# Delta stage of a small Perceiver block: triangular solve by doublings, filters as matrix products

## The reference, cut to what matters

```
q, k, v = silu(conv4(hs @ Wq)), silu(conv4(hs @ Wk)), silu(conv4(hs @ Wv))   # causal, per channel
beta = sigmoid(hs @ Wb);  q, k = l2norm(q), l2norm(k)                     # per head
A = tril_strict((k * beta) @ k.T);  u = inv(I + A) @ (v * beta) ...       # chunks of 32, state S
delta = tril(q @ k.T) @ u                                                 # the same, unchunked
local_short, local_long = fir5(v), fir64(v)                               # causal, per channel
stats = [mean, var, mean|.|, l2] of local_short, local_long, delta, v     # 16 per token and head
logits = gelu([hs, stats] @ mlp_w1 + b1) @ mlp_w2 + b2;  p = softmax(logits / temp) * 0.84 + floor
o = p0 * local_short + p1 * local_long + p2 * delta + p3 * v + sigmoid(res) * local_short
out = (o * rsqrt(mean(o * o) + 1e-5) * rms_w) @ Wo
```

## Time and profile before

| | us |
|---|---|
| three runs | 453.78, 455.37, 457.92 (median 455.37) |
| the profiled execution | 456.18 |
| its span | 454.1 |
| start of the delta stage (xn turned, L696) | 393.42 |
| x after it (L1648) | 439.13 |

### The profile page before, as it was taken

The page is one execution under the profiler, slowest core; times in us unless marked ns, Lnnn a source line. Parts: engine busy times, 40 slices in busy tenths (PEclk is TensorE's granted clock), DMA queues, the critical chain, the costliest instruction groups (busy, mean ns, idle before and its releaser), DMA issues.

```text
span 454.1 us, 11496 instructions
## 1 busy us (share of the span) xinstructions
PE 406.9 (90%) x4493; PEld 321.3 (71%) x4493; DVE 341.5 (75%) x927; ACT 286.5 (63%) x558; POOL 220.4 (49%) x141
## 2 busy tenths in 40 slices
PE   6988999999989999989888999999999999874776
PEld 3956777777767788889656776777776889753575
DVE  2688888888877886447599989888888764488653
ACT  3366888888878876334187897988898651260220
POOL 1177879878845620010014698874665100169110
PEclk9799999999999999999999999999999999995989
DMA  8689897989999889600049999999999900000000
GB/s 321 254 230 177 146 168 134 178 155 219 167 227 238 178 149 398 243 0 5 1 89 192 168 191 191 188 174 193 197 188 194 157 4 1 1 0 0 2 0 3
DMA packets 185781, 64.95 MB, mean 143 GB/s; under 512 B 181168, under 2 KB 181376, under 8 KB 184960
## 3 DMA queue, kind: packets, MB, share of 16 engines
q1 hardware_dynamic: 185440, 63.18, 70.2%
q10 hardware_dynamic: 288, 1.05, 0.7%
HBM read 18.76 MB, written 0.03 MB: 41 GB/s over the span
## 4 chain that ended last, share of the span: by engine, by line
PE 32%; DVE 31%; POOL 10%; ACT 8%; issue 8%; DMA 8%; SPq 2%; DVEq 0%; POOLq 0%; ACTq 0%
DVE probs L563 13%; PE ps L475 9%; DMA probsT<-halves 7%; PE ps L443 7%; PE ps L690 4%; ACT probs L507 4%; POOL halves L539 3%; DVE probsT L592 3%; ACT halves L514 2%; DVE U L581 2%; POOL moe L1244 2%; PE ps L455 2%; PE ps L976 2%; SPq L395 2%; DVE den L576 1%
## 5 line engine op out<-in xcount | busy, mean ns | idle before, releaser
L539 POOL TENSOR_TENSOR halves<-probs,halves 128x896 f16<-128x896 f32 x67 | 126.5, 1891 | 83.4 <-ACT halves L514 82.6
L443 PE MATMUL ps<-ctxT_parts,GT_parts 128*128 128x512 f16 (+1 forms) x672 | 145.4, 353 | 11.5 <-DVE negmax L563 9.5
L475 PE MATMUL ps<-ctxN,probsT 128*128 128x128 f16 x2352 | 149.3, 219 | 6.5 <-DMA probsT<-halves 4.0
L475 PEld LDWEIGHTS ps<-ctxN,probsT 128*128 128x128 f16 x2352 | 139.2, 98 | 21.0 <-issue 6.1
L507 ACT ACTIVATE probs<-probs,shifted 128x896 f32<-128x896 f32 x112 | 115.5, 1032 | 12.3 <-DVE shifted L568 12.3
L443 PEld LDWEIGHTS ps<-ctxT_parts,GT_parts 128*128 128x128 f16 x672 | 60.2, 98 | 63.8 <-DVE negmax L563 14.3
L514 ACT CAST halves<-probs 128x896 f16<-128x896 f32 x92 | 84.9, 923 | 0.1
L563 DVE CUSTOM_DVE_ANT_0 probs<-ps,zero,negmax 128x896 f32<-128x896 f32 x56 | 67.5, 1205 | 1.5 <-PE ps L443 1.3
L563 DVE CUSTOM_DVE_ANT_0 probs<-ps,maskb,negmax 128x896 f32<-128x896 f32 x56 | 67.5, 1205 | 1.2 <-POOL halves L539 0.7
L581 DVE SCALAR_TENSOR_TENSOR U<-U,alpha,ps 128x128 f32<-128x128 f32 x112 | 38.4, 343 | 32.8 <-PE ps L475 32.6
L690 PE MATMUL ps<-cst 128*128 128x128 f32 x454 | 61.5, 286 | 0.0
(11 more groups left out here) (347 smaller groups left out, 388.8 us busy)
## 6 DMA issues: line engine op xcount, KB each, us to landing
moe<-in_ctxT SPq DMA_DIRECT2D x7, 448.0 KB, 8.1
moe<-in_mask SPq DMA_DIRECT2D x6, 448.0 KB, 10.8
moe<-in_gateT SPq DMA_DIRECT2D x2, 1024.0 KB, 9.3
moe<-in_upT SPq DMA_DIRECT2D x2, 1024.0 KB, 10.8
moe<-in_downT SPq DMA_DIRECT2D x2, 1024.0 KB, 12.7
probsT<-halves SPq DMA_TRANSPOSE x92, 4.7
wv<-in_wv SPq DMA_DIRECT2D x2, 512.0 KB, 4.9
wo<-in_wo SPq DMA_DIRECT2D x2, 512.0 KB, 5.7
```

The source lines that it names most:

```text
L443: ins = pe.matmul(ps[:, 2 * b + h, 0:width], GT_parts[:, g_part, r * P:(r + 1) * P], ctxT_parts[:, keys:keys + width], start=(g_part == 0 ...
L475: ins = pe.matmul(ps[:, bank, 0:D], probsT_parts[:, b, p_part, k * P:(k + 1) * P], ctxN_parts[:, at:at + D], start=(p_part == 0 and c_part ...
L539: eng.tensor_tensor(halves_of(L, n)[:, 1, :], probs[:, n % BUFS, :], halves_of(L, n)[:, 0, :], ALU.subtract).then_inc(lower_of(L, n)[0], 1)
```

## The change

The convolution's taps are multiplied into Wq, Wk and Wv by one GpSimd product, so that q, k and v come out of 12 products over shifted columns of xn (`conv`). The solve uses two partition halves of 64 tokens, two heads each: six levels, in each of which TensorE multiplies the right-hand side and the key matrix by one factor (`hop_x`) and the next factor out of the key matrix (`hop_y`); ScalarE copies the one, VectorE the other under a mask. The filters are products with diagonal matrices that are loaded after the second attention pass (`fir`), the long one spread between the levels by `FIR_AT`. Branches lie on 128 partitions (64 tokens, two sides of two heads), 64 columns each, and the statistics of v and the short filter are taken between the levels, those of the delta and the long filter after them. Tanh takes the place of Exp for beta, and Silu's table is asked for ahead. On GpSimd the identity copy for the factors is at step 30 of the second pass, the weights' product after it. Cut to its core:

```
 
 GATE_BANKS, DOWN_BANKS = (2, 3, 4, 5), (6, 7, 0, 1)
 WARM = [0, 2, 6, 6, 6, 6]
...
 for _name, _width in [("ident", P), ("ones", P), ("block32", P), ("later", S), ("upto", S), ("head8", AH),
...
+            pe.wait_ge(sem("d_convw"), 1)
+
+            def conv(i, bank, col):
+                for k in range(TAPS):
+                    for side in range(2):
+                        rows = slice(side * S, (side + 1) * S)
+                        ins = pe.matmul(ps[rows, bank, col:col + S], conv_w[:, i, k, rows], xpad[:, k:k + S],
+                                        start=(k == 0), stop=(k == TAPS - 1))
+                return ins
+
+            def fir(first, last):
+                for k in range(first, last):
+                    for side in range(2):
+                        rows = slice(side * S, (side + 1) * S)
+                        ins = pe.matmul(ps[rows, 7, 0:S], vpad[rows, k:k + S], fir_long[rows, k, :], start=(k == 0),
+                                        stop=(k == FIR_L - 1))
+                return ins
...
+            def by_head(bank, left, right):
+                for h in range(DH):
+                    dims, side = slice(h * DD, (h + 1) * DD), h // 2
+                    ins = pe.matmul(ps[side * S:(side + 1) * S, bank + h % 2, 0:S], left[dims, :], right[dims, :],
+                                    start=True, stop=True)
+                return ins
+
+            def hop_y(level):
+                for a in range(2):
+                    for side in range(2):
+                        rows = slice(side * S, (side + 1) * S)
+                        ins = pe.matmul(ps[rows, 1, a * S:(a + 1) * S], X[rows, a, DD:], LT[rows, level, a, :],
+                                        start=True, stop=True)
+                ins.then_inc(sem("d_hop"), 1)
...
+            def hop_x(level, right, width):
+                for a in range(2):
+                    for side in range(2):
+                        rows = slice(side * S, (side + 1) * S)
+                        ins = pe.matmul(ps[rows, 0, a * width:(a + 1) * width], LT[rows, level, a, :],
+                                        right[rows, a, 0:width], start=True, stop=True)
+                return ins
...
+            conv(0, 0, 0)
+            conv(1, 0, S).then_inc(sem("d_given"), 1)
+            for side in range(2):
+                rows = slice(side * S, (side + 1) * S)
+                pe.matmul(ps[rows, 1, S:2 * S], W("wb")[:, rows], xpad[:, TAPS - 1:], start=True, stop=True)
+            conv(2, 1, 0).then_inc(sem("d_given"), 1)
+            stay_warm(pe, 6, 2)
+            pe.wait_ge(sem("d_dve"), D_DVE["sq"])
+            pe.matmul(ps[:, 2, 0:2 * S], C("block32"), sq, start=True, stop=True).then_inc(sem("d_given"), 1)
...
+            pe.wait_ge(sem("d_act"), D_ACT["v"])
...
+            for side in range(2):
+                rows = slice(side * S, (side + 1) * S)
+                pe.matmul(ps[rows, 6, 0:S], vpad[rows, FIR_L - 1:], ident[rows, rows], start=True, stop=True)
...
+                    rows = slice(side * S, (side + 1) * S)
+                    at = FIR_L - FIR_S + k
+                    ins = pe.matmul(ps[rows, 6, S:2 * S], vpad[rows, at:at + S], fir_short[rows, k, :], start=(k == 0),
+                                    stop=(k == FIR_S - 1))
+            ins.then_inc(sem("d_given"), 1)
...
+            for side in range(2):
+                rows = slice(side * S, (side + 1) * S)
+                ins = pe.matmul(ps[rows, 5, 0:S], R[rows, :], ident[rows, rows], start=True, stop=True)
+            ins.then_inc(sem("d_given"), 1)
+            fir(0, FIR_AT[0])
+            pe.wait_ge(sem("d_dve"), D_DVE["kbeta"])
+            by_head(3, qkh[:, 1, :], kbneg).then_inc(sem("d_given"), 1)
+            by_head(0, kbneg, qkh[:, 1, :]).then_inc(sem("d_given"), 1)
+            fir(FIR_AT[0], FIR_AT[1])
+            for level in range(LEVELS - 1):
+                pe.wait_ge(sem("d_lt"), level + 1)
...
+                hop_y(level)
+                hop_x(level, X, DD + S if level < LEVELS - 2 else DD).then_inc(sem("d_hop"), 1)
+                if level == 0:
+                    pe.wait_ge(sem("d_dve"), D_DVE["qhat"])
+                    by_head(3, qkh[:, 1, :], qkh[:, 0, :]).then_inc(sem("d_given"), 1)
+                fir(FIR_AT[level + 1], FIR_AT[level + 2])
+            pe.wait_ge(sem("d_lt"), LEVELS)
+            pe.wait_ge(sem("d_x"), LEVELS)
+            hop_x(LEVELS - 1, w, DD).then_inc(sem("d_given"), 1)
+            fir(FIR_AT[LEVELS], FIR_AT[LEVELS + 1])
+            pe.wait_ge(sem("d_dve"), D_DVE["bm"])
+            pe.wait_ge(sem("d_x"), LEVELS + 1)
...
+                    ins = pe.matmul(ps[rows, 2, a * DD:(a + 1) * DD], Bm[rows, a, :], u_s[rows, a, :], start=True,
+                                    stop=True)
+            ins.then_inc(sem("d_given"), 1)
+            fir(FIR_AT[LEVELS + 1], FIR_L).then_inc(sem("d_given"), 1)
+            stay_warm(pe, 0, 8)
...
+            pe.matmul(ps[:, 4, 0:DH * S], d_w[:, 4 * D:5 * D], xpad[:, TAPS - 1:].unsqueeze(1).broadcast_to([P, DH, S]),
+                      start=True, stop=False)
+            pe.wait_ge(sem("d_stats"), 2)
...
-            pe.matmul(ps[:, 1, 0:S], W("wb"), xnT[:, 0:S], start=True, stop=True).then_inc(sem("d_given"), 1)
...
-            for g in range(8):
...
-                pe.matmul(ps[:, g, 0:8 * w], C("block32"), Z[:, g, 0:8 * w], start=True,
...
-                pe.matmul(ps[0:S, 2, D:2 * D], firp[:, :, k], ident, start=(k == 0), stop=(k == 3))
...
-
...
-            for g in range(1, 8):
-                key_products(pool, g).then_inc(sem("d_z"), 1)
...
-            pseq(pool.tensor_tensor(firp[:, :, 0:rest], windows(vpad, rest),
-                                    W("fir_l")[:, 0:rest].unsqueeze(1).broadcast_to([P, S, rest]), ALU.mult))
...
-            while width > 4:
-                pseq(pool.tensor_tensor(firp[:, :, 0:width], firp[:, :, 0:width], firp[:, :, width:2 * width], ALU.add))
...
+                        if n == 30:
+                            pool.tensor_copy(LT.rearrange("p l a t -> p (l a) t"),
+                                             C("pairs")[:, 0:S].unsqueeze(1).broadcast_to([P, 2 * LEVELS, S])).then_inc(
+                                sem("d_lt_ident"), 1)
+                    loaded(pool, "delta", "conv")
+                    pool.wait_ge(sem("o1T_ready"), 1)
+                    pool.tensor_tensor(conv_w, conv_w, d_w[:, 0:3 * D].rearrange("p (i d) -> p i d", i=3).unsqueeze(
+                        2).broadcast_to([P, 3, TAPS, D]), ALU.mult).then_inc(sem("d_convw"), 1)
...
+            act.activation(sres[:, 1, :], W("res"), ACT.Exp, scale=-1.0).then_inc(sem("d_early"), 1)
+            loaded(act, "delta")
+            act.activation(w1s[:], w1s[:], ACT.Copy, scale=C("w1scale", slice(0, 16))).then_inc(sem("d_early"), 1)
...
-            act.activation(vpad[:, FIR_L - 1:], cv[:, 2, :], ACT.Silu).then_inc(sem("d_v"), 1)
-            act.wait_ge(sem("d_nrm"), 1)
-            act.activation(rn.rearrange("p a t -> p (a t)"), nrm, ACT.Sqrt).then_inc(sem("d_sqrt"), 1)
...
-            for k in range(FIR_L - ACT_TAPS, FIR_L):
-                a = PARAM["fir_l"][0] + k
-                act.activation(firp[:, :, k], vpad[:, k:k + S], ACT.Copy,
-                               scale=par[:, a:a + 1]).then_inc(sem("d_taps"), 1)
...
+            act.activation(spare[:], C("power"), ACT.Silu)
...
+            act.activation(qkc.rearrange("p a t -> p (a t)"), ps[:, 0, 0:2 * S], ACT.Silu).then_inc(sem("d_act"), 1)
...
+            act.activation(vpad[:, FIR_L - 1:], ps[:, 1, 0:S], ACT.Silu).then_inc(sem("d_act"), 1)
+            act.activation(tb, ps[:, 1, S:2 * S], ACT.Tanh, scale=0.5).then_inc(sem("d_act"), 1)
+            act.wait_ge(sem("d_given"), D_GIVEN["norm"])
+            act.activation(rn.rearrange("p a t -> p (a t)"), ps[:, 2, 0:2 * S], ACT.Sqrt,
...
+            act.wait_ge(sem("d_given"), D_GIVEN["vb"])
+            act.copy(X[:, :, 0:DD], ps[:, 5, 0:S].rearrange("p (a d) -> p a d", a=2))
+            act.wait_ge(sem("d_given"), D_GIVEN["gram"])
+            act.copy(X[:, :, DD:], ps[:, 0:2, 0:S]).then_inc(sem("d_x"), 1)
+            for level in range(LEVELS - 2):
+                act.wait_ge(sem("d_hop"), 2 * level + 2)
+                act.copy(X.rearrange("p a c -> p (a c)"), ps[:, 0, 0:2 * (DD + S)]).then_inc(sem("d_x"), 1)
+            act.wait_ge(sem("d_hop"), 2 * LEVELS - 2)
+            act.copy(w.rearrange("p a c -> p (a c)"), ps[:, 0, 0:2 * DD]).then_inc(sem("d_x"), 1)
             act.wait_ge(sem("d_brcopied"), 1)
...
-            act.activation(st[:, :, :, 3].rearrange("p h b -> p b h"),
-                           mom[:, 2, :].rearrange("p (b h) -> p b h", b=4), ACT.Sqrt).then_inc(sem("d_stats"), 1)
+            act.activation(sqs[:, 0:2, :], br[:, 0:2, :], ACT.Square).then_inc(sem("d_squares"), 1)
+            act.wait_ge(sem("d_given"), D_GIVEN["u"])
```

(91 more changed lines are left out.)

297 lines of the change are left out of this document (105 added, 192 removed).

## The result

| | before | after |
|---|---|---|
| median of four runs, us | 456.41 | 437.97 |
| lowest and highest | 453.78, 457.92 | 437.51, 438.64 |
| the profiled execution, and its span | 456.18, 454.1 | 437.51, 435.4 |
| xn turned (start) | 393.42 | 392.66 |
| transposes of the statistics (start) | 429.50 | 411.52 |

The ratio of after to before is 0.9603 [0.9552, 0.9654]. Between the profiled executions 18.7 us are gone: 17.9 in the stage (46.00 us from xn turned to the addition's end, now 28.07), and 0.76 ahead of it.

The account below looks back on a forecast made before the run. Two chains ending together, GpSimd's long filter and VectorE's substitution, were taken as the bound. 18.8 us gained, less 0.3 for the identity copy and 0.5 for tile switches, gave 18.0: 456.18 to 438.2, range 434.5 to 445.5.

Parts of the forecast that it names:

- kbneg ready: End of the convolution and norm part: kbneg at 399.0 where the old kernel has 401.25, 2.2 us gained.
- Diagonal tiles: Filter products on TensorE: two 64x64 tiles laid diagonally overlap, 0.117 us a pair, with 0.23 kept for the range.
- rival of 448.8: Filter pairs on TensorE: diagonal tiles go one after the other at 0.23 a pair, 10.6 us together; chance 0.08.
- that of 470: Filter pairs between levels: tiles in series at the low clock, 0.46 a pair, slower than before; chance 0.03.
- Tile shapes: TensorE's switches of tile shape, five on the path: 0 to 0.5 us, 0.5 taken.
- Tanh and Silu's table: ScalarE in the convolution: tanh needs no table load (0, else 1.28); loading Silu's table ahead covers 1.28 us.
- Shortening one alone would give nothing: Old delta stage: GpSimd's filter chain and VectorE's substitution end together, so cutting only one gains nothing.
- The change removes both: Old delta stage: the change takes away both GpSimd's filter chain and VectorE's 63 substitution steps.
- rival of 446: TensorE from level 0 on: the clock falls, doubling the same terms, some 8 us; chance 0.05.
- Moved work: Identity copy in the second pass 0 to 1.6 us, 0.3 taken; weights' product 3.1, hidden; added loads nothing.
- Levels: Solve's levels: 1.2 us each from products, latency, ScalarE's copy and hand-overs, with five filter pairs free.
- rival of 442: Levels and statistics: slower hand-overs, 0.5 us more a level and 1 in the statistics; chance 0.14.

Follow-up runs that it names:

- a_byside: Changed kernel with the long filter's products issued all of side 0, then all of side 1, per group: 0.976 of the kernel before, 445.25 us, stage 4.48 longer.
- a_tail: Changed kernel with 46 of the long filter's 64 pairs behind the last level: 0.9726 of the kernel before, stage 34.76 us, 4.87 longer.
- a_nosilu: Changed kernel without the early request for Silu's table: 0.9613 of the kernel before, stage 29.88 us, no change.
- b_nofilter: Kernel before without GpSimd's multiply for 48 long-filter taps and its additions by halves: ratio 0.9999, stage 47.23 us, 0.59 shorter.
- b_half: Kernel before with 31 of the 63 substitution steps: ratio 1.0077, stage 50.38 us, 2.56 longer.
- b_both: Kernel before with 31 of 63 substitution steps and without GpSimd's 48 long-filter taps: ratio 0.9972, stage 45.74 us, 2.08 shorter.
- b_order: b_both with TensorE's branch products ahead of its last substitution wait, 18 idle products between, four later ones removed: 0.9837 of the kernel before, 447.44 us, stage 38.60.
- a_onetap: Changed kernel with one tap of the long filter instead of 64: 0.9617 of the kernel before, stage 30.29 us, 0.40 longer.
- b_half_warm: Kernel before with 31 substitution steps, full filter, b_order's TensorE order and 48 idle products: ratio 1.0063, stage 47.52 us, 0.30 shorter.
- a_onetap_warm: Changed kernel with one long-filter tap and idle products (five before the products by head, two per level): 0.9609 of the kernel before, stage 28.93 us, 0.96 shorter.

## Why the prediction was right

The forecast was 438.2, measured 437.97. By its own steps, with its clock (xn turned and ready at 393.75) moved back by 0.72, to 393.03, where the copy of xn starts in the changed kernel:

| step | predicted | measured |
|---|---|---|
| kbneg ready | 398.28 | 398.28 |
| products by head start | 398.63 | 398.96 |
| first level starts | 399.88 | 399.89 |
| period of a level | 1.20 | 1.28 |
| u copied | 406.7 | 407.03 |
| statistics ready | 410.43 | 410.93 |
| transposes, with the 0.5 for tile shapes | 411.28 | 411.52 |
| transposes to the addition's end, less than before | 0.8 | 0.71 |

The mechanism is right, but the last few tenths are luck. The stage was forecast to lose 18.3 us (18.8 less 0.5) and lost 17.93; ahead of it 0.3 more was forecast, and 0.76 less came, which scatter explains as well (last section). Inside the stage, the products by head start 0.33 late, and the first level starts 0.93 behind them, not 1.25: their records are shorter than the 0.06 us allowed (16 in 0.46 us). The two errors cancel in the third row.

- **Diagonal tiles.** Right, and the step that decides. 72 filter records, all of them into bank 7, both halves of the partitions, take (2.27 - 0.22) / 71 = 0.029 each, 0.115 a pair, where 0.117 was taken. a_byside shows the other end of the range, 0.056 for neighbours on one tile, and what it costs: 4.48 us of the stage. The Trainium skill's rule (TensorEngine Tiling (Array Packing), Gotcha 1) that different row tiles cannot access one PSUM bank at the same time does not hold for tiles that differ in rows and columns: the measurement decides. The rival of 448.8 fell with it, and that of 470.
- **Tile shapes.** The last of 72 filter records began at 396.76 + 2.27 - 0.22 = 398.81 and the products by head 0.15 later, where neighbours of one shape follow at 0.03: 0.12 for a change between tiles of 64 and of 32 rows. Three such changes lie on the path: one ahead of the products by head, two in the first level, where TensorE's queue has no gap. That is 0.36, inside the range of 0 to 0.5, of which the upper end was taken. The one behind the products by head is off the path: the first level waits for VectorE's masked copy and starts 0.94 behind the products by head in a_tail too, which has no filter there.
- **Tanh and Silu's table.** Tanh needed no load: right. That the early request covers 1.28 us: **wrong**, as a_nosilu shows; nothing is lost without it.
- **The bound of the old kernel.** "Shortening one alone would give nothing": right, by b_nofilter and by b_half, which even lost. "The change removes both", as the full reason: **incomplete**. b_both removes both and gains 2 us. The change gains 18 because it also takes away TensorE's own chain of branch products behind its wait for the substitution, and the low clock in which they ran; b_order, with half the substitution and all of that out of the way, gets 9.2, 7.1 of them by the third chain. Of the other 8.7, 8.0 lie ahead of the transposes (27.85 us after the power that begins the stage in b_order, 19.86 in the changed kernel), 2.2 of them in the convolution: kbneg is ready 6.62 after that power, 8.84 in the kernel before, the 2.2 of the prediction. I had seen the clock of 0.54 and priced it as a danger for the new kernel alone, not as a part of what bounded the old one. The sum was right all the same, since it followed the new chain and didn't subtract pieces of the old.
- **Clock.** The rival of 446 did not come: 1.00 up to 411, then 0.83 under short work. a_onetap and a_tail show how near it was: each has gaps that the filter fills in the changed kernel, and their stages came out 1.8 and 1.7 us above what was expected of them from prices at a clock of 1.00. In a_tail 1.6 of that is the last filter records: 128 more of them took 5.28 us more, 3.7 at 0.029 each.
- **Moved work.** The identity copy took 0.83, not 1.6, and fell into an idle time that is 2.04 after it: nothing on the path. The product of the weights took 3.44, not 3.1, under cover: nothing. The second pass's last 12.2 stayed 12.2 (356.61 to 368.81). From the power ahead of the second pass to the one that begins the stage it took 0.20 more (173.57 for 173.37), where 0.3 was taken. One pair of profiles can't show that: the eight with the identity copy lie between 172.81 and 173.73 (mean 173.27), the six without between 172.65 and 173.37 (mean 172.97).
- **Levels.** A period from 402.75: the eight and eight records end at 403.53, ScalarE's copy runs 403.57 to 403.89, the next product starts at 404.03. Products 0.78 (0.75 taken), copy 0.32 (0.37), hand-overs 0.18 (0.1), so the rival of 442, slower hand-overs with 0.5 more a level, did not come. The masked copy cost 0.30, the plain copy's end of its bounds.

## What to carry to other kernels

Where two engines' chains end together, look for a third on the engine that waits for both: write its queue out from the wait to the end, at the clock of that stretch. To price a rewrite, follow the new chain instruction by instruction against the clock of the old trace, and don't subtract what is removed. Work that fills a gap of TensorE can be free twice over, since it also holds the clock; before you take it or an idle product out, ask what fills its place.

## What was not expected of the hardware

- Two 64x64 fp32 tiles on the diagonal run at once into one bank: 0.029 us a record if the tiles take turns, 0.056 if neighbours share one. Records to other tiles of the array go between them (a_byside, from 406.91).
- ScalarE loads a table as soon as its queue gets to the instruction, ahead of the semaphore wait: 388.51 for a Silu at 394.28.
- With 8.6 us less on VectorE a kernel got 2.6 us longer in its stage, because TensorE's gap moved and the clock with it.
- The start of the kernel has two speeds. From 15.4 to 19.6 and to 23.4, with the same instructions, before:

```profile
15.40:19.60 4.20, 4.10 (x46) 3.90 (x46) 2.09 (x9) 1.04 (x1) 0.00 (x0) 0.89 0.75 294
19.60:23.40 3.80, 2.75 (x24) 2.56 (x23) 3.55 (x10) 0.69 (x1) 2.91 (x2) 1.00 0.17 39
```

and b_half_warm:

```profile
15.40:19.60 4.20, 4.11 (x35) 3.60 (x33) 2.29 (x9) 1.22 (x3) 0.00 (x0) 0.50 0.73 286
19.60:23.40 3.80, 3.80 (x20) 3.80 (x19) 0.94 (x4) 0.00 (x0) 0.27 (x1) 0.50 0.00 0
```

At 0.50 the scores of the first pass start at 26.28, not 23.46. In the fourteen profiles of this study that start lies between 20.98 and 26.28, in kernels of both kinds. Not all of it is the clock: in a_onetap_warm, the earliest, the products ahead of it (L739) already begin at 12.50, where the kernel before (L714) has 15.40. The 0.76 that the changed kernel gained ahead of the stage is 0.54 at this start and 0.84 in the first pass, less 0.42 in the expert stage and 0.20 in the second pass. Each of the first three scatters by as much or more among the profiles of one kind, so how much of the 0.76 the change gave is not shown.

Nor is it shown that the clock is most of what separates single runs, though the executions of the kernel before speak for it: of 46, the ten shortest (453.8 us in the mean) have a mean granted clock of 0.981, the ten longest (458.3) one of 0.972.
